# Channel attention in a gated two-layer kernel: no zero rows through DRAM, a fourth bank of first scores, and output blocks in two halves

## The reference, cut to what matters

```python
q, k, v = Wq @ (norm(x)*mask) + bq, Wk @ (ctx*mask) + bk, Wv @ (ctx*mask) + bv   # 128 rows: 16 heads x 8
scores[h] = q_h.T @ k_h / sqrt(8)        # 256 x 256 a head, masked with -1e6
out[h] = softmax(scores[h]) @ v_h        # then x = x + tanh(g_xattn) * out * mask
```

## Time and profile before

| What | us |
|---|---|
| Median of 3 runs | 1765.13 (1763.63 to 1768.89) |
| The profiled execution | 1769.25 |
| Its span | 1766.8 |
| TensorE busy in the span | 1665.2 (94%) |
| VectorE busy | 1115.3 (63%) |
| ScalarE busy | 969.2 (55%) |
| 256 maxima (L1275), idle before them | 164.7, 51.0 |
| 256 exponentials (L979), idle before them | 138.6, 75.7 |

### The profile page before, as it was taken

The page is one execution under the profiler, slowest core; times in us unless marked ns, Lnnn a source line. Parts: engine busy times, 40 slices in busy tenths (PEclk is TensorE's granted clock), DMA queues, the critical chain, the costliest instruction groups (busy, mean ns, idle before and its releaser), DMA issues. The chain is left out here.

```text
span 1766.8 us, 33713 instructions
## 1 busy us (share of the span) xinstructions
PE 1665.2 (94%) x11512; PEld 1399.9 (79%) x11520; DVE 1115.3 (63%) x2501; ACT 969.2 (55%) x2463; POOL 591.1 (33%) x654
## 2 busy tenths in 40 slices
PE   7969987798899999999999999999999997899997
PEld 6635554458798898888988898898898996789986
DVE  6758867798556656756667655555555567854434
ACT  2648865585545545545556645545545543655543
POOL 6235535544522112112122211111111212877774
PEclk9889988799999999999999999999999999899999
DMA  7467662102100100100100021001000005443438
GB/s 234 113 134 180 162 186 94 40 27 101 52 13 13 37 13 13 47 0 12 37 25 25 13 65 37 13 1 36 12 0 13 1 1 130 140 117 114 132 117 284
DMA packets 68571, 122.84 MB, mean 70 GB/s; under 512 B 12424, under 2 KB 45496, under 8 KB 67442
## 3 DMA queue, kind: packets, MB, share of 16 engines
q1 hardware_dynamic: 59845, 98.36, 19.5%
q0 software_dynamic: 7584, 21.37, 4.1%
q10 hardware_dynamic: 1000, 1.26, 0.2%
HBM read 87.48 MB, written 32.88 MB: 68 GB/s over the span
## 5 line engine op out<-in xcount | busy, mean ns | idle before, releaser
L2518 POOL TENSOR_TENSOR hold_wq<-hold_wq,ca_rsum 128x512 f32<-128x512 f32 x128 | 134.0, 1047 | 795.3 <-DVE ca_rsum L2760 795.3
L2378 ACT ACTIVATE hold_wq<-ca_pT 128x512 f32<-128x512 f32 x128 | 76.4, 597 | 377.8 <-PE ca_pT L2585 377.8
L1275 DVE TENSOR_REDUCE a_mx<-a_s 128x2 f32<-128x512 f32 x256 | 164.7, 686 | 51.0 <-PE a_s L1107 49.4
L979 ACT ACTIVATE a_prob<-a_s 128x512 f32<-128x512 f32 x256 | 138.6, 596 | 75.7 <-PE a_s L1127 74.2
L2741 DVE COPY ca_values<-ca_v 128x512 f32<-128x512 f32 x128 | 88.3, 690 | 125.5 <-PE ca_v L2537 124.9
L2535 PE MATMUL ca_qk<-early_x,cw_wqkv_h 128*128 128x512 f32 x384 | 160.9, 419 | 1.3 <-PEq L1737 1.3
L2750 DVE TENSOR_TENSOR hold_wq<-ca_s,hold_wk 128x512 f32<-128x512 f32 x128 | 88.3, 690 | 104.7 <-PE ca_s L2578 104.6
L2537 PE MATMUL ca_qk<-early_x,cw_wqkv_l 128*128 128x512 f32 x384 | 151.6, 395 | 0.0
L2536 PE MATMUL ca_qk<-early_x,cw_wqkv_h 128*128 128x512 f32 x384 | 151.1, 393 | 0.0
L2658 PE MATMUL ca_acc<-ca_wo_h,ca_oT_l 128*128 128x256 f32 x512 | 145.0, 283 | 0.0
L2657 PE MATMUL ca_acc<-ca_wo_l,ca_oT_h 128*128 128x256 f32 x512 | 144.7, 283 | 0.0
(11 more groups left out here) (562 smaller groups left out, 4580.8 us busy)
## 6 DMA issues: line engine op xcount, KB each, us to landing
a_qks<-a_strips SPq DMA_DIRECT2D x52, 256.0 KB, 4.7
early_big<-slot_results SPq DMA_DIRECT2D x16, 512.0 KB, 9.2
a_strips<-a_hi SPq DMA_DIRECT2D x26, 256.0 KB, 4.0
mw_raw<-in_d_expert_w SPq DMA_DIRECT2D x12, 352.0 KB, 4.8
a_strips<-a_low SPq DMA_DIRECT2D x13, 256.0 KB, 3.8
mw_down<-in_d_expert_d SPq DMA_DIRECT2D x1, 2816.0 KB
a_wraw<-a_heads SPq DMA_DIRECT2D x17, 128.0 KB, 2.0
token_rows<-early_rows SPq DMA_DIRECT2D x1, 2176.0 KB, 16.5
```

The costliest lines, as they stand in the source:

```text
L979: act.activation(prob[:, w % PR, :, :], s2_bank(w)[:, :, :], ACT.Exp, scale=1.0 / A_ROOT)\
L1275: dve.tensor_reduce(mx[:, b % 2, :, h], s1_bank(b, u)[:, :, :], AX.X, ALU.max)\
```

## The change

There are three edits, all in `attend_channels`.

1. The zero rows no longer go through DRAM. `send_zeros` is gone; GpSimd clears the one strip buffer that batch 3 is the first to use (the other three hold stacked batches, whose rows 28 to 31 are zero), and `load_strips` reads 28 of the 32 rows. In SP's queue the maxima of batch 0 now stand ahead of the masks.
2. A fourth bank of first scores: from use 40 on (batch 2, from unit 5) they rotate over proj[1] and the three s1 banks. The values, which used proj[1], move to proj[0], both halves in slot 13; their bias product waits until the low part of the last join has been read.
3. `weigh` is split into its two halves of four matmuls. The first stands one slot earlier, in the double slots 0, 4, 8, 12; the second in 2, 6, 10, 14 as before.

```diff
         def values(t):
+            return built(t) if built(t) is not None and built(t) >= WHOLE_ROWS and t % U == VALUES else None
...
         def weighed(t):
-            w = t - A_LAG - 3
-            if w >= SLOW:
-                w = w - 1 if w >= SLOW + 1 else -1
-            return (w // U, w % U // A_SLOTS) if 0 <= w < ALL and w % A_SLOTS == A_SLOTS - 1 else None
+            halves = []
+            for half in range(2):
+                w = t - A_LAG - (2 + half)
+                if w >= SLOW or w - half >= SLOW:
+                    w = t - A_LAG - 4
+                    if w < SLOW:
+                        continue
+                if 0 <= w < ALL and w % A_SLOTS == A_SLOTS - 1:
+                    halves.append((w // U, w % U // A_SLOTS, half))
+            return halves
...
-        JOIN, VALUES, MASKED, ZEROED = 8, (5, 13), 4, 6
+        JOIN, VALUES, MASKED = 8, 13, 4
+        FILLED_ROWS = 28
...
-            return (5 * b + ORDER.index(f"{kind}{part}")) % 2 if b < WHOLE_ROWS else 1
+            return (5 * b + ORDER.index(f"{kind}{part}")) % 2 if b < WHOLE_ROWS else 0
...
                 if kind == "v":
-                    eng.wait_ge(k_stack, 2 * WHOLE_ROWS)
-                    eng.wait_ge(v_ready, b)
+                    eng.wait_ge(qk_lo, min(b + 2, BATCHES) - WHOLE_ROWS)
                 else:
-                    eng.wait_ge(v_ready, WHOLE_ROWS)
+                    eng.wait_ge(v_ready, max(WHOLE_ROWS, b - 1))
...
+        WIDE = (U + 1) * (WHOLE_ROWS - 1) + 6
+        WIDER = [proj[1]] + [s1[(WIDE + k) % S1_BANKS] for k in range(S1_BANKS)]
+        def use_bank(use):
+            return s1[use % S1_BANKS] if use < WIDE else WIDER[(use - WIDE) % len(WIDER)]
...
-                def send_zeros(a, b):
-                    for k in range(2):
-                        sp.dma_start(strips[a:b, 4 * k + 3, P // 2:P, :],
-                                     mext[a:b, 0:DIM].bitcast(F32).unsqueeze(1).broadcast_to([b - a, P // 2, DIM]))\
-                          .then_inc(zeros_sent, 16)
...
-                        sp.dma_start(qks[A_ROWS * r:A_ROWS * r + A_ROWS, :, b % A_BUFS, :, :]
-                                     .rearrange("p k j n -> p k (j n)").bitcast(F32), image[r]).then_inc(strip_in[p], 16)
+                        sp.dma_start(qks[A_ROWS * r:A_ROWS * r + FILLED_ROWS, :, b % A_BUFS, :, :]
+                                     .rearrange("p k j n -> p k (j n)").bitcast(F32), image[r, 0:FILLED_ROWS])\
+                          .then_inc(strip_in[p], 16)
+                maxima(0)
                 send_masks()
-                maxima(0)
-                send_zeros(WHOLE_ROWS, ZEROED)
                 maxima(1)
...
-                    if b == 1:
-                        send_zeros(ZEROED, BATCHES)
...
+                    pool.memset(qks[:, :, A_BUFS - 1, :, :].bitcast(F32), 0.0).then_inc(pads_ready, 1)
...
-                    if weighed(t):
-                        weigh(*weighed(t))
+                    for half in weighed(t):
+                        weigh(*half)
...
+                    if values(t) is not None:
+                        project_v(values(t), 0)
+                        project_v(values(t), 1)
...
-                        if value_half(t) and value_half(t)[0] >= WHOLE_ROWS and value_half(t)[1] == 0:
-                            bias_v(value_half(t)[0])
+                        if values(t) is not None:
+                            bias_v(values(t))
```

More of the change, by code:

```diff
@@ L514, in value_half, with values @@
             b, u = built(t), t % U
-            if b is None or u not in (VALUES if b >= WHOLE_ROWS else (13, 15)):
+            if b is None or b >= WHOLE_ROWS or u not in (13, 15):
                 return None
-            return b, (VALUES if b >= WHOLE_ROWS else (13, 15)).index(u)
+            return b, (u - 13) // 2
+        def values(t):
+            return built(t) if built(t) is not None and built(t) >= WHOLE_ROWS and t % U == VALUES else None
         def values_read(t):
@@ L522, in values_read @@
                 return t // U
-            return built(t) if built(t) is not None and built(t) >= WHOLE_ROWS and t % U == VALUES[1] + 1 else None
+            return built(t) if built(t) is not None and built(t) >= WHOLE_ROWS and t % U == VALUES + 1 else None
         def turned(t):
@@ L963, in read_maxima @@
                     use = (U + 1) * (b + 1) + TURN_USE
[L964 removed]
+                    act.activation(mT[:, b % 2, :], use_bank(use)[0:A_HEADS, 0, :], ACT.Copy, scale=-1.0)\
                         .then_inc(mT_ready, 1)
@@ L1136, in turn_maxima, with weigh @@
                     for t in range(2):
-                        mm = pe.transpose(s1[use % S1_BANKS][0:A_HEADS, 0, P * t:P * t + P], mx[:, b % 2, t, :], ident[:, :])
+                        mm = pe.transpose(use_bank(use)[0:A_HEADS, 0, P * t:P * t + P], mx[:, b % 2, t, :], ident[:, :])
                     mm.then_inc(mT_psum, 1)
-                def weigh(b, j):
-                    pe.wait_ge(prob_ready, U * b + A_SLOTS * (j + 1))
+                def weigh(b, j, t):
                     o = out_bank(b, j // 2)
-                    if j == 0:
-                        pe.wait_ge(v_ready, b + 1)
-                    if b == 0 and j == 0:
-                        pe.wait_ge(work.gram_lo, work.grams_to(0))
-                    if j % 2 == 0 and o is proj[0]:
-                        pe.wait_ge(work.gram_lo, work.grams_to(2))
-                    if j % 2 == 0 and o is not out:
-                        pe.wait_ge(qk_lo, BATCHES - WHOLE_ROWS)
-                        pe.wait_ge(v_ready, BATCHES)
-                    if j % 2 == 0 and o is out:
-                        after(pe, out_copied, 2 * b + j // 2 if b < BATCHES - 1 else 2 * b - 1)
-                    for t in range(2):
-                        for v in range(A_SLOTS):
-                            r = (v + 2) % A_SLOTS
-                            mm = pe.matmul(o[A_ROWS * r:A_ROWS * r + A_ROWS, j % 2, :],
-                                           vT[:, b % A_BUFS, t, A_TILES * r + j, :],
-                                           prob[:, (U * b + A_SLOTS * j + v) % PR, t, :], start=(t == 0), stop=(t == 1),
-                                           skip_group_check=True)
-                    mm.then_inc(out_psum, 1)
@@ new lines, in weigh @@
+                    if t == 0:
+                        pe.wait_ge(prob_ready, U * b + A_SLOTS * (j + 1))
+                        if j == 0:
+                            pe.wait_ge(v_ready, b + 1)
+                        if b == 0 and j == 0:
+                            pe.wait_ge(work.gram_lo, work.grams_to(0))
+                        if j % 2 == 0 and o is proj[0]:
+                            pe.wait_ge(work.gram_lo, work.grams_to(2))
+                        if j % 2 == 0 and o is not out:
+                            pe.wait_ge(qk_lo, BATCHES - WHOLE_ROWS)
+                            pe.wait_ge(v_ready, BATCHES)
+                        if j % 2 == 0 and o is proj[1]:
+                            pe.wait_ge(mT_ready, BATCHES)
+                        if j % 2 == 0 and o is out:
+                            after(pe, out_copied, 2 * b + j // 2 if b < BATCHES - 1 else 2 * b - 1)
@@ new lines, in weigh @@
+                    for v in range(A_SLOTS):
+                        r = (v + 2) % A_SLOTS
+                        mm = pe.matmul(o[A_ROWS * r:A_ROWS * r + A_ROWS, j % 2, :],
+                                       vT[:, b % A_BUFS, t, A_TILES * r + j, :],
+                                       prob[:, (U * b + A_SLOTS * j + v) % PR, t, :], start=(t == 0), stop=(t == 1),
+                                       skip_group_check=True)
+                    if t == 1:
+                        mm.then_inc(out_psum, 1)
```

17 lines of the change are left out of this document (9 added, 8 removed).

## The result

The kernel after takes 1777.77 us, the median of 19 runs (1768.71 to 1796.4); before, timed beside it, 1764.59 (1756.99 to 1771.15). The ratio is 1.0069, 95% interval [1.005, 1.0087]: slower by 0.7%, where 1759 and a gain were forecast and the range ended at 1769. The profiled execution took 1778.91, its span is 1777.0.

The account below looks back on a forecast made before the run. ScalarE's loop over two banks of second scores was taken to bound steady batches, 1.63 us a pair. Terms -17.1 + 13.2 + 0 - 1.4 - 1.1 = -6.4 us gave 1762.9 profiled, 1759 for the median; range 1745 to 1769.

Parts of the forecast that it names:

- term 1: SP's queue before the hi parts: without the zero rows the stall between two exponentials goes, gain 17.1 us.
- join: Pair of slots 8 and 9: half a block behind the q and k products makes it 2.18 us, 0.55 longer, 12 times.
- values: Pair of slots 12 and 13: waiting for VectorE's low part and a half block make it 2.59 us, 0.96 longer.
- term 4: Steady batches: the six other pairs fall to 1.63 us; a batch becomes 14.55 against 13.45, +13.2 us over 12.
- rival B: Slower: TensorE waits for VectorE in each batch and the granted clock falls, three falls giving 1771 us; chance 0.12.
- Term 5: SP's queue: masks behind the maxima of batch 0 may delay batch 1's maxima; taken as 0, from 0 to 3 us.
- Rival A: Steady batches: the bank of first scores bounds them, so the fourth bank brings 1731 us; chance 0.13.
- Rival C: SP's queue: the stall moves to maxima and strips behind the masks, up to 10 us return, 1769 us; chance 0.11.

Follow-up runs that it names:

- e1: The kernel before with edit 1 alone (no zero rows through DRAM), masks still ahead of the maxima of batch 0: 1751.23 us, ratio 0.990.
- h5: e1 with ScalarE computing the tenth exponential of each batch 1 to 12 twice: 1769.37 us, ratio 1.0014.
- h3: e1 with ScalarE computing the sixth exponential of each batch 1 to 12 twice: 1776.98 us, ratio 1.0072.
- h4: e1 with a short ScalarE copy and wait between the two exponentials of six pairs of each batch 1 to 12: 1781.17 us, ratio 1.0078.
- e2: The kernel after with the masks sent ahead of the maxima of batch 0 again: 1778.17 us, ratio 1.0077.
- h2: g3 with the mask rows sent ahead of the maxima of batch 0: 1766.1 us, ratio 1.0008.
- h6: h1 with all six value products in the pair of slots 4 and 5: 1744.53 us, ratio 0.9858.
- e4: The kernel before with edits 1 and 3 (no zeros, half blocks), three banks of first scores, masks first: 1760.38 us, ratio 0.9968.
- e3: The kernel after with each block of output products whole again (edits 1 and 2): 1765.2 us, ratio 0.9987.
- h7: h6 with batch 3's value products alone moved to slots 12 and 13: 1743.35 us, ratio 0.9863.
- g3: The kernel after with the value products in two halves, in slots 3 and 5, instead of all in slot 13: 1761.08 us, ratio 0.9985.
- h0: Against the kernel before: no zero rows, whole blocks, values in slots 3 and 5 of one projection bank, the freed bank empty: 1764.77 us, ratio 0.9972.
- h1: h0 with the freed bank used as a third bank of second scores: 1746.08 us, ratio 0.9893.
- g1: e1 with ScalarE computing two exponentials (second and sixth) of each batch 1 to 12 twice: 1806.98 us, ratio 1.0238.

## Why the prediction was wrong

**Right.** The stall and its cause (term 1: -17.1, and e1). The pairs: join 2.07 against 2.18, values 2.53 against 2.59, the wait for the low part 0.24 against 0.23, the half block 0.57 against 0.55, the others 1.63 to 1.69; batch 14.63 against 14.55. The 1.69 behind a block stayed, which term 4 had let go; join and values came out 0.17 cheaper and made up for most of it. On these grounds I had the change as a gain of 6. At the end of the channel attention the forecast is 18.1 us off: 12.2 are the half level in the steady batches, 4.9 the opening, 1.0 the length of the batch.

**The step that failed** is the one that set rival B aside, and with it left the clock in the steady batches out of the sum, a term of 0 where 12.2 us were measured: "the clock was 1.00 over eight batches whose weight loads idled 26.1 us". This shows that the clock held at 13.45 us a batch, not how far it was from falling. h5 and h3 measured that: half a microsecond of waiting more in a batch, and it spends a third (0.84) to a good half (0.73) of the nine batches at the half level. The mechanism was written down, with its price (4 us a fall, three falls: 1771), and in the profile three falls between 106 and 251 us cost 144.29 - 9 x 14.63 = 12.6 us. That this is about three times 4 is luck: the half level lasts 34.2, 10.2 and 6.8 us behind the three, and by the batches in which they lie they cost 8.3, 2.7 and 1.7. The price goes by the time at the half level, in this profile a quarter of a microsecond for each, not by the fall. Rival B was given 0.12 where its condition, TensorE waiting once more in each batch, was part of my own forecast. A forecast that lengthens a loop bounded by another engine had to carry the clock in its sum.

A warning was there to be read as well. The Trainium skill, TensorE: Matmul & The Clock Gate, A second HAM failure mode: psum-queue depth-cycling, says of another kernel, in bf16 with 512 columns, that short idle times between groups of matmuls, where PSUM banks are cycled, make the clock go up and down. This loop waits for its banks in each double slot, and the traces of after, h3, h4 and h5 agree (clocks of 0.82, 0.73, 0.82 and 0.84). But the loops of before and e1 wait there as well and kept 1.00, so the warning alone doesn't say which of these kernels falls.

**Mis-sized.** Term 5 was taken at 0: the maxima did go out at 67.33, as worked out, and were awaited 3.27 us; batches 0 and 1 cost 4.9 in all. The wait behind the masks was 2.5 us; what the term left out is that from the issue to TensorE's start another 5.4 us pass, and the use was due at 69.48, 4.7 us behind the making and not 6.5. e2 and h2 show that the other order isn't better. Why the openings differ (42.5 us in h6, 45.5 in e1, 52.6 in after, 56.8 in e4) isn't settled; the half level stands in it for 7 and 9 us in the two short ones, for 14 and 41 in the two long ones (e4's from an execution 10 us above its median).

**Rival A** (the bank of first scores bounds) fell with e3: four banks and whole blocks give 13.63. Rival C was there in small: 3.27 us, in the maxima of batch 1 alone.

Not settled either is which property of a stretch lets the clock fall. TensorE's busy share doesn't tell: 0.94 in after's 161 to 213 us, from which it fell, 0.85 in h7's nine batches (97.46 of 114.91), in which it didn't.

## What to carry to other kernels

A change that lets TensorE wait longer in a loop that repeats is to be priced twice, at full clock and with the granted clock fallen; 0.5 us of waiting in 13.5 was enough in h5 to cost more than itself (the nine batches grew by 18.6 us, of which 4.3 are the waiting), while e4 and g3, 0.54 and 0.42 longer by more and moved work of TensorE, kept the clock in their profiles. Before splitting a block for a smoother order, look at what else lands in that pair of slots: the split cost 12.6 us in medians (e3 to after), and with six value products spread over two pairs 16.7 came back (after to g3). And a bank that comes free was worth more in the loop that sets the pace, which ScalarE's constant 1.63 us named in the profile of before: as a third one of second scores it gave 18.7 us (h0 to h1).

## What the runs showed of the hardware

- At the half level TensorE had no idle time in 34.10 us and the level stayed for all of it (after, 127.3 to 161.4); being busy is not enough to bring it back. The Trainium skill, TensorE: Matmul & The Clock Gate, Part 1, has a busy engine back at full clock soon; by this row the measurement decides against it for this mix of work, mostly tiles of 32 rows or columns.
- ScalarE got 1.26 us more a batch in g1 and the nine batches grew by 43.6 us: with the clock, a delay on another engine cost almost four times its 11.3 us.
- Eight writes of mask rows kept SP's queue for 18.3 to 18.8 us of issue alone, whether they stood behind the maxima of batch 0 (after) or ahead of them (before, e1, e2, h2, h7).
- A half block of eight matmul instructions costs 0.57 us of TensorE's time (after, 192.43 to 193.00), a whole one of sixteen 1.00 (before, 141.73 to 142.73).
- Each microsecond at the half level cost this loop about a quarter of a microsecond (after: 12.6 us for 51.2 in the nine batches).
